# Edge types in eight bins of 63 with overlapping pairs of bins, in place of four quarters of 125

## The reference

```
m    = clifford_linear(h_hc[src] * r_hc[edge_type], msg_w, msg_b)
gate = sigmoid(r_uv @ gate_w.T + gate_b)
m    = m * gate * norm
h_agg = segment_sum(m, dst)          # 206250 edges -> 6250 nodes
```

## Time and profile before

| | us |
|---|---|
| median of 3 runs | 5540.87 (5525.53 to 5540.95) |
| the profiled execution | 5538.96 |
| its span, first to last instruction | 5537.2 |
| first gather of pass one, of pass two | 245.4, 2799.0 |
| last gather of pass one, of pass two | 2766.3, 5436.3 |

### The profile page before, as it was taken

How to read it: one execution, slowest core, us unless ns; L and a number is a source line. 1 busy time by engine, 2 the same in 40 slices (tenths; PEclk the granted TensorE clock), 3 DMA queues, 4 the chain that set the end, 5 groups by cost and what they waited for, 6 DMA issues and landing times.

```text
span 5537.2 us, 71370 instructions
## 1 busy us (share of the span) xinstructions
PE 3935.6 (71%) x21018; PEld 3039.0 (55%) x21018; DVE 3031.5 (55%) x11695; ACT 1615.8 (29%) x6417; POOL 3854.6 (70%) x4302
## 2 busy tenths in 40 slices
PE   6555555555655566555568888888888888888886
PEld 6444444444444444444445666666666666666665
DVE  8845555555555555555545554545545454555545
ACT  3144544445444454454400111111111111111111
POOL 0177777777777777777767777777777777777772
PEclk9577777777777777777789999999999999999998
DMA  4333333333333333333344444444444444444442
GB/s 97 117 94 96 98 97 96 97 96 98 97 96 98 97 96 97 98 96 93 97 110 114 112 112 109 113 106 112 109 111 111 109 112 108 109 110 115 108 108 76
DMA packets 275026, 571.67 MB, mean 103 GB/s; under 512 B 86332, under 2 KB 164377, under 8 KB 274643
## 3 DMA queue, kind: packets, MB, share of 16 engines
q0 software_dynamic: 164640, 456.82, 32.9%
q1 hardware_dynamic: 98162, 101.78, 5.9%
q10 hardware_dynamic: 11840, 8.50, 0.5%
HBM read 539.92 MB, written 26.92 MB: 102 GB/s over the span
## 4 chain that ended last, share of the span: by engine, by line
PE 40%; DVE 31%; another core or an unknown queue 17%; issue 8%; ACT 2%; DMA 1%; SPq 0%; DVEq 0%; PEldq 0%; ACTq 0%
PE psE L707 15%; DVE both L1335 8%; PE psT L688 7%; PE psY L688 6%; DVE work L1409 5%; DVE work L1405 4%; PE psE L901 3%; PE psE L882 2%; ACT work L1073 2%; DVE work L1257 2%; PE psY L664 1%; DVE work L1352 1%; DVE work L1343 1%; DVE st L1466 1%
## 5 line engine op out<-in xcount | busy, mean ns | idle before, releaser
L601 POOL DMA_INDIRECT work<-t_d,srci x3430 | 3276.2, 955 | 1581.8 <-issue 1166.2
L707 PE MATMUL psE<-work,both 128*128 128x257 f32 x6860 | 2172.1, 440 | 796.7 <-issue 308.0
L707 PEld LDWEIGHTS psE<-work,both 128*128 128x128 f32 x6860 | 1364.0, 221 | 1131.1 <-issue 391.1
L1073 ACT ACTIVATE work<-work 128x35 f16<-128x35 bf16 x5145 | 1131.8, 311 | 657.0 <-DVE work L1405 440.7
L1335 DVE TENSOR_SCALAR both<-iof,dstf 128x128 f32<-128x128 f32 x3430 | 817.4, 347 | 29.6 <-remote 16.4
L1405 DVE TENSOR_SCALAR work<-iob,work 128x35 bf16<-128x35 bf16 x1715 | 273.2, 267 | 870.3 <-remote 692.3
L1352 DVE TENSOR_TENSOR work<-work,psT 128x257 f32<-128x257 f32 x858 | 347.4, 420 | 632.4 <-PE psT L688 276.3
L1352 DVE TENSOR_TENSOR work<-work,psY 128x257 f32<-128x257 f32 x857 | 347.3, 420 | 622.8 <-PE psY L688 231.3
L598 POOL MEMSET idle<- 128x640 bf16 x856 | 574.0, 671 | 0.2
L688 PE MATMUL psT<-relb,work 125*128 125x257 bf16 x3381 | 541.8, 283 | 19.5 <-DVE work L1343 18.5
L688 PE MATMUL psY<-relb,work 125*128 125x257 bf16 x3381 | 545.4, 284 | 4.5 <-issue 4.3
(11 more groups left out here) (260 smaller groups left out, 3218.2 us busy)
## 6 DMA issues: line engine op xcount, KB each, us to landing
work<-t_d,srci POOLq DMA_INDIRECT x3430
work<-types_d SPq DMA_DIRECT2D x245, 218.8 KB
both<-acc_d SPq DMA_DIRECT2D x98, 130.0 KB
t_d<-accf SPq DMA_DIRECT2D x7, 910.0 KB, 9.1
acc_d<-work ACTq DMA_DIRECT2D x1, 6370.0 KB
t_d<-accf SPq DMA_DIRECT2D x49, 130.0 KB
X<-in_x SPq DMA_DIRECT2D x1, 6144.0 KB
out<-X SPq DMA_DIRECT2D x6, 896.0 KB
```

The lines of the kernel that those rows point to most:

```text
L601: pool.indirect_dma_start(gath[:, n % RG, :], None, table, bass.IndirectOffsetOnAxis(ap=srci[:, n:n + 1], axis=0)).then_inc(s_g[n % RG], 16)
L707: ins = nc.tensor.matmul(psE[:, b % 2, 0:DW], sel[:, third, k % SG, :], gath[:, n % RG, 0:DW], start=False, stop=(k == C - 1))
L1073: ins = nc.scalar.activation(to_s3[:, n % 2, i, j, :], to_s[:, n % 2, i, :], ACT.Copy, scale=load3[:, b // RB % 2, j, w:w + 1])
```

## The change

The types are sorted into BINS = 8 bins of BIN = 63 types (the last has 59) and not into 4 quarters of 125. The relation table is held as PAIRS = 7 overlapping pairs of neighbouring bins, each pair on PT = 126 partitions (types 63c to 63c + 125), again in three bfloat16 parts. A slot that holds edges of two neighbouring bins is then served by one pair. Counted from the planning functions: before, 539 of the 1715 slots have two visits and the total is 2254; in the changed kernel 2 slots have two and the total is 1717. A visit is three matmuls in both. The one-hot instructions of pass two go from 395 to 493, over 1717 x 128 columns in all where there were 2254 x 128.

What else comes with it:

- `marks` makes 8 masks in place of 4 and finds the bin by a multiplication and a shift.
- `rank` and `places` go block by block, since 8 x 35 = 280 columns of three blocks do not fit a PSUM bank. A new semaphore `s_pl` lets TensorE write the next block's counts only when VectorE has read the last.
- In the group loop a batch is a period of 15 groups. Its steps stood at group 11 (`marks`), 12 (`rank`) and 14 (`places`) of the period before; they stand at 5 (`marks`), 6, 9 and 12 (`rank`), and 9, 12 and 14 (`places`).
- The bfloat16 parts of the table are no longer made ahead of pass one. The gated table goes to DRAM as before; SP loads one pair at a time back into `gw` (`load_pair`, at blocks 3, 7, ..., 27) and VectorE splits it (`parts`, at group 0 of blocks 6, 10, ..., 30).
- `within` tests 7 borders and not 3. `relb` grows by 3 pairs, and to make room `idle`, `digits`, `turn_at` and `st` move or shrink. The memset between gathers has the same shape in a new place.

The core of the diff:

```
-def quarters(b, k):
+def pairs(b, k):
     first = [0] + [lo for lo, hi in turns(b)]
     end = [hi for lo, hi in turns(b)] + [C]
-    return [c for c in range(RK) if first[c] <= k < end[c]]
+    has = [c for c in range(BINS) if first[c] <= k < end[c]]
+    odd = len(has) % 2 and has[-1] == PAIRS
+    return list(range(has[0] - odd, has[-1] + 1, 2))
...
-        relb = sb("relb", [P, 3, RK, DW + 1], BF16)
-        tid = sb("tid", [P, RK])
+        relb = sb("relb", [P, 3, PAIRS, DW + 1], BF16)
+        tid = sb("tid", [P, PAIRS])
...
+            def load_pair(c):
+                q = min(PT, R - BIN * c)
+                if c == 0:
+                    sp.wait_ge(s_relwd, 16)
+                else:
+                    sp.wait_ge(s_split, c)
+                sp.dma_start(gw[0:q, 0:DW], relw_d[BIN * c:BIN * c + q, :]).then_inc(s_pair, 16)
...
-            def rank(r):
-                w = blocks_of(r) * RK * C
-                pe.wait_ge(s_rk, r + 1)
...
+            def rank(b):
+                pe.wait_ge(s_rk, b // RB + 1)
+                if b >= 1:
+                    pe.wait_ge(s_pl, b)
+                if b >= 2 * RB:
+                    pe.wait_ge(s_typ_h, b // RB - 1)
+                mine = marked[:, b % RB, :, :].rearrange("p c k -> p (c k)")
+                nc.tensor.matmul(psT[:, 0, 0:BINS * C], trib[:, :], mine, start=True, stop=True)
+                nc.tensor.matmul(psT[:, 1, 0:BINS * C], oneb[:, :], mine, start=True, stop=True).then_inc(s_rp, 1)
...
-            dve.wait_ge(s_relwd, 16)
-            for part in range(3):
-                link(v.tensor_copy(relb[0:q, part, :, 0:DW], rel_sb[0:q, :, :]))
-                if part < 2:
-                    link(v.tensor_tensor(rel_sb[0:q, :, :], rel_sb[0:q, :, :], relb[0:q, part, :, 0:DW], ALU.subtract))
+            v.memset(relb[:, :, PAIRS - 1, :], 0.0)
...
+            def parts(c):
+                q = min(PT, R - BIN * c)
+                dve.wait_ge(s_pair, 16 * (c + 1))
+                for part in range(3):
+                    ins = v.tensor_copy(relb[0:q, part, c, 0:DW], gw[0:q, 0:DW])
+                    if part < 2:
+                        link(ins)
+                        link(v.tensor_tensor(gw[0:q, 0:DW], gw[0:q, 0:DW], relb[0:q, part, c, 0:DW], ALU.subtract))
+                ins.then_inc(s_split, 1)
...
+            def places(r, i):
+                b, nb = RB * r + i, blocks_of(r)
+                m, at = BINS * C, C * i
+                dve.wait_ge(s_rp, b + 1)
+                flat = before[:, :, :].rearrange("p c k -> p (c k)")
+                mine = marked[:, i, :, :].rearrange("p c k -> p (c k)")
+                link(v.tensor_tensor_scan(flat, ones[:, 0:1].broadcast_to([P, m]), psT[:, 1, 0:m], 0.0, ALU.mult, ALU.add))
+                link(v.tensor_tensor(flat, flat, psT[:, 1, 0:m], ALU.subtract))
+                link(v.tensor_copy(turn_at[:, b, :], before[:, 1:BINS, 0]))
+                link(v.tensor_tensor(flat, flat, psT[:, 0, 0:m], ALU.add))
+                dve.sem_inc(s_pl, 1)
+                link(v.tensor_tensor(flat, flat, mine, ALU.mult))
+                link(v.tensor_reduce(spot[:, at:at + C], before[:, :, :].rearrange("p c k -> p k c"), AX, ALU.add))
+                if i < nb - 1:
+                    return
...
-                        b, g = n // SPB, n % SPB
-                        if b % RB == RB - 1 and b + 1 < NB:
-                            if g == 1:
-                                marks(b // RB + 1)
-                            if g == 4:
-                                places(b // RB + 1)
+                    for r in range(1, RANKS):
+                        if n == SPB * RB * (r - 1) + 5:
+                            marks(r)
+                        for i, j in zip(range(blocks_of(r)), (9, 12, 14)):
+                            if n == SPB * RB * (r - 1) + j:
+                                places(r, i)
+                    for c in range(PAIRS):
+                        if n == SPB * (4 * c + 6):
+                            parts(c)
```

More of the change, by code:

```diff
@@ L48 @@
 RP = R // RK
+BINS = -(-R // BIN)
+PAIRS = BINS - 1
+PT = 2 * BIN
+TO_BIN = -(-(1 << 16) // BIN)
 HT = H // P
@@ L69, in turns @@
     out = []
-    for j in (1, 2, 3):
-        f = j / 4
+    for j in range(1, BINS):
+        f = j * BIN / R
         spread = 4 * sqrt(n * f * (1 - f) + n * f * f)
@@ L87, in visits @@
     out, at = [], 0
-    for c in range(RK):
-        has = [i for i in range(SG) if c in quarters(b, SG * g + i)]
-        if has:
-            out.append((c, has[0], len(has), at))
-            at += len(has)
+    for c in range(PAIRS):
+        i = 0
+        while i < SG:
+            many = 0
+            while i + many < SG and c in pairs(b, SG * g + i + many):
+                many += 1
+            if many:
+                out.append((c, i, many, at))
+                at += many
+            i += many + 1
     return out
@@ L127, in program @@
         accf = sb("accf", [P, NB * W])
-        work = sb("work", [P, 11604])
+        work = sb("work", [P, 11404])
         srci = sb("srci", [P, SLOTS], I32)
@@ L146, in program @@
         o = RG * W
-        H4 = work[:, o:o + 2 * RW].bitcast(BF16).rearrange("p (b c k) -> p b c k", b=RB, c=RK)
-        o += 2 * RW
-        before = work[:, o:o + 4 * RW].rearrange("p (b c k) -> p b c k", b=RB, c=RK)
-        o += 4 * RW
+        marked = work[:, o:o + BINS * RW // 2].bitcast(BF16).rearrange("p (b c k) -> p b c k", b=RB, c=BINS)
+        o += BINS * RW // 2
+        before = work[:, o:o + BINS * C].rearrange("p (c k) -> p c k", c=BINS)
+        o += BINS * C
         good = work[:, o:o + RW]
@@ L235, in program @@
         f2 = work[:, o:o + HT * D].rearrange("p (t n) -> p t n", t=HT)
-        assert o + HT * D <= 11604
+        o += HT * D
+        assert o + 320 <= 11404
+        idle = [accf[:, NB * W - 320:NB * W].bitcast(BF16), work[:, o:o + 320].bitcast(BF16)]
         late = typ[:, :].bitcast(F32)
@@ L254, in program @@
         iob = sb("iob", [P, P], BF16)
-        idle = sb("idle", [P, 640], BF16)
         w1s = sb("w1s", [P, 2, D])
@@ L351, in program @@
         s_rp = sem("s_rp")
+        s_pl = sem("s_pl")
+        s_pair = sem("s_pair")
+        s_split = sem("s_split")
         s_t1 = sem("s_t1")
@@ L544, in _ @@
             for b in range(NB + 2):
+                if b % 4 == 3 and b // 4 < PAIRS:
+                    load_pair(b // 4)
                 if b + 1 < NB:
@@ L597, in gathers @@
                             pool.wait_ge(s_pause, pause - 1)
-                        pool.memset(idle[:, :], 0.0).then_inc(s_pause, 1)
+                        pool.memset(idle[layer], 0.0).then_inc(s_pause, 1)
                     if n >= RG:
@@ L687, in relations @@
                     for part in range(3):
-                        ins = nc.tensor.matmul(psR[n % BANKS][:, 0:DW], oht[0:RP, g % 2, at, :], relb[0:RP, part, c, 0:DW],
+                        ins = nc.tensor.matmul(psR[n % BANKS][:, 0:DW], oht[0:PT, g % 2, at, :], relb[0:PT, part, c, 0:DW],
                                                start=((c, part) == (mine[0][0], 0)), stop=((c, part) == (mine[-1][0], 2)))
@@ L734, in first_pass @@
             def first_pass():
-                rank(0)
+                for i in range(RB):
+                    rank(i)
                 for n in range(NB * SPB + SPB + 6):
@@ L738, in first_pass @@
                     if n < NB * SPB:
-                        if b % RB == RB - 1 and b + 1 < NB and g == 2:
-                            rank(b // RB + 1)
                         for i in range(SG):
                             aggregate(0, SG * n + i)
+                    for r in range(1, RANKS):
+                        for i, j in zip(range(blocks_of(r)), (6, 9, 12)):
+                            if n == SPB * RB * (r - 1) + j:
+                                rank(RB * r + i)
                     if 0 < n <= NB * SPB:
@@ L971, in _ @@
             first_pass()
-            pe.wait_ge(s_rp, RANKS)
+            pe.wait_ge(s_pl, NB)
+            pe.wait_ge(s_split, PAIRS)
             pe.wait_ge(s_so, NB)
@@ L1342, in one_hots @@
                 for c, first, many, at in visits(n):
-                    ins = v.tensor_scalar(oht[0:RP, n % 2, at:at + many, :], types[0:RP, n % 2, first:first + many, :],
-                                          tid[0:RP, c:c + 1], None, ALU.is_equal)
+                    ins = v.tensor_scalar(oht[0:PT, n % 2, at:at + many, :], types[0:PT, n % 2, first:first + many, :],
+                                          tid[0:PT, c:c + 1], None, ALU.is_equal)
                 ins.then_inc(s_oht, 1)
@@ L1374, in marks @@
                 link(v.tensor_tensor(load3[:, r % 2, 2, 0:w], t, ok, ALU.mult))
[L1376 to L1391 removed]
+            def places(r, i):
[13 more added lines that the diff above has]
+                    return
+                w = C * nb
                 link(v.tensor_copy(src_a[:, 0:w], spot[:, 0:w]))
@@ L1415, in first_pass @@
```

(3 more changed lines are left out.)

68 lines of the change are left out of this document (28 added, 40 removed).

## The result

Over 19 runs each on one chip the changed kernel takes 5525.80 us (5503.03 to 5546.23) and the kernel before 5536.73 (5525.53 to 5547.51): ratio 0.9982 [0.9974, 0.9991], a gain of some 10 us or 0.2%. The forecast was 5511, a gain of 28. The profiled execution after is 5539.22 us with a span of 5537.5, some 13 above the median of its own kernel. So the two traces show no difference in the total, and only their parts can be compared.

A forecast was written before the change was run, and what follows sets the result against it. The prediction took both passes to be bound by GpSimd's gathers, plus an 8% tax from TensorE falling behind. From the profiled 5539 us it summed 5539 - 45 + 15 + 1 + 1 = 5511 us, range 5425 to 5575.

The forecast's parts named there:

- the tax: Both passes: time per slot above GpSimd's burst floor, from TensorE falling behind; 0.128 us in pass one, 0.125 in pass two.
- pass two's term, -45: Pass two: 537 fewer visits lighten TensorE by 3.6 us per block, so the pace falls and 45 us go.
- The rounding up from 39 to 45: Pass two: 39 us in proportion, taken as 45 because the first microseconds off TensorE should be worth more.
- 3.6 us per block: Pass two: TensorE time saved by fewer visits, 0.33 us each and 11 per block of 35 slots.
- the stretch without feed-forward: Pass two, 2830 to 2980 us: 7.7 us less TensorE work per block lowers the pace from 1.545 to 1.493.
- Pass one at +15: Pass one: longer sorting on VectorE, chiefly `marks` ahead of `features` at group 5, costs 1 us per batch, 16 times.
- +1 and +1: Start: table split leaves, longer sorting and the accumulator's load cancel it, +1 us; end: `within` grows by 16 instructions, +1.
- The hand-over to `rank`: Pass one: `rank` of a batch's second and third block waits for VectorE's `s_pl`, under 1 us each.
- `places` was put at 3.0 us: Pass one: `places`, 4.1 us once per batch before, now runs three times at 3.0 us, 9.0 in all.
- The first: Rival, pass two: quicker draining of TensorE's backlog takes 130 of 198 us of lateness; 5426 us, chance 0.13.
- The third: Rival, pass one: `marks` ahead of `features` passes 4.8 us per batch to GpSimd, +77 us; 5571 us, chance 0.18.
- The second: Rival, pass two: VectorE's lumps or a falling TensorE clock eat the gain; 5549 us, no change, chance 0.24.

The follow-up runs named there:

- e18: The kernel before without its second visits on TensorE, sorting and one-hots as before, on the slower kind of chip: 5511.51 us, 0.9953 of the kernel before.
- e4: The changed kernel with the 537 second visits done again on TensorE, the result the same: 5461.13 us, 1.0019 of the kernel before.
- e1: The changed kernel with `marks`, `places` and `parts` at the end of VectorE's group and later `rank` one group later: 5444.25 us, 0.9983 of the kernel before.
- e2: The changed kernel with `marks` alone moved to the end of VectorE's group: 5442.73 us, 0.9976 of the kernel before.
- e17: The changed kernel with only the first of the three bfloat16 parts multiplied, on the slower kind of chip: 5477.97 us, 0.9879 of the kernel before.
- e14: The kernel before with twelve gathers to a burst in both passes: 5546.00 us, 1.0162 of the kernel before.
- e15: The changed kernel with twelve gathers to a burst in both passes: 5580.71 us, 1.022 of the kernel before.
- e13: The kernel before with six gathers to a burst in pass two in place of three: 5512.92 us, 1.0101 of the kernel before.
- e16: The changed kernel with six gathers to a burst in pass two in place of three: 5494.84 us, 1.007 of the kernel before.
- e3: The kernel before with `marks` moved to group 5, ahead of `features`: 5457.21 us, 1.0001 of the kernel before.
- e7: The kernel before, unchanged, run again for a profile on a chip of the faster kind: 5149.56 us, one run.

## Why the prediction was wrong

On a chip with the tax both parts moved as forecast in sign. The size of the gain in pass two did not hold, and the whole gain fell from 28 us to 10.

- **The step that failed: the size of pass two's term, -45.** Measured, the visits are worth 26 us (e18; 17 to 35), 17 to 23 by e4 beside e1 and e2, 36 by the two traces of pass two, and none where the gathers run at their floor. With 26 in place of 45 the forecast's own sum gives a gain of 9 us, and 10 was measured. That a lighter TensorE makes pass two faster on such a chip was right. Two parts of the term were too large. The rounding up from 39 to 45, by which the first microseconds are worth more, had no row behind it, and no such effect is seen in the returns of e17 and e18. And the relief was counted in matmuls at full clock, 3.6 us per block. TensorE's busy time per slot went from 1854.60 / 1391 = 1.333 us to 1776.95 / 1412 = 1.258 with the change and to 1766.29 / 1407 = 1.255 in e18, which is only 2.7 us per block. The matmuls that stayed got longer: one of an aggregate takes 408 ns on average before, 416 with the change, 418 in e18 and 439 in e17 (3250 to 5300 us), at a granted clock of 0.94, 0.93, 0.92 and 0.87. With 2.7 the same proportion gives 0.052 x 2.7 / 7.7 x 1582 = 29 us, an estimate inside e18's interval. So the comparison with the stretch without feed-forward is not refuted, but it was a thin basis: from start to start of the gathers the two stretches lie 0.024 to 0.072 us per slot apart in the 12 traces of the slower kind. (The 131 instructions of the changed kernel can't be divided by 150 us, since its pass two begins at 2835 and not at 2830.)
- **Pass one at +15, with +1 and +1.** All of the change but the visits costs 10 us by e4, and 26 - 10 = 16 by e18 and the result. Single traces scatter: pass one from first to last gather is longer with the changed sorting by 37 us in the pair of the result, 31 between e18 and e17, 22 between e14 and e15, 7 between e13 and e16 and 2 between e3 and e4. The term was about right, the reason beside it was not: it was put down to 1 us per batch of lumps that fall through at group 5. e3 put the old lump there and lost nothing, and e2 took the new one away and gained nothing that can be told. The hand-over to `rank` was put at under 1 us each and is some 8 us when it is seen, but e1, which has none of it, is no faster than e2. Which of the added steps costs the 10 to 16 us is open. `places` was put at 3.0 us and takes 3.2.
- **The tax.** The prediction said that GpSimd's floor is the bound and that the tax is TensorE's falling behind "now and then". Both hold, and the parts of the tax, 0.128 and 0.125 us per slot or 220 and 214 us, are near the 200 and 175 us by which a chip without it is faster. What was not asked is why TensorE falls behind. Pauses between moves that have no wait between them were in the trace of the kernel before as well, and would have warned that load is not all of it. That load only sets how fast TensorE recovers from such a stretch is an argument; no run shows it.
- **The rivals.** The first (the tax nearly goes with quicker draining) falls with e17: with three times the relief in all, pass two is still at 1.492. The third (`marks` ahead of `features`) falls with e1 to e3. The second came nearest of the three in time, 5549 against 5526, but the visits did bring a gain, which it had eaten. That VectorE's lumps set the rest of the tax was not tested. The granted clock of pass two went from 0.94 to 0.93, and not to 0.76; in e17 it is 0.87 with TensorE 75% busy, and that kernel is 57 us faster than the changed one. The rule of the Trainium skill (TensorE: Matmul & The Clock Gate, section on HAM oscillation), that pauses bring the low rate back, agrees in direction with 0.94, 0.93, 0.87. What the low rate costs is seen in the longer matmuls of the first point: it took back part of the relief, not all of it.
- **What would show it.** 5150 relation matmuls: 5151. Pace of pass two 1.517: 1.522. Clock 0.92 or above: 0.93. Pace of pass one 1.475: 1.490. Waits moved to the features' transposes: 34 to 81 us. The pace of pass two in the one profiled run bore the forecast out better than the runs did: by the medians the gain is a third of it.

Still open: what makes TensorE and VectorE issue slowly in some sets, whether that is of the chip or of the recording, how much of the tax it accounts for, and why denser gathers make the tax larger. No run tells whether a deeper ring or finer freeing helps there.

## What to carry to other kernels

When an engine falls behind now and then, look in the trace at a run of its instructions that have no wait between them: if they stand far apart, its load is not all of the lateness, and lightening it may return only a fraction (here some 0.15 us per us). Price what an edit takes from TensorE in busy time and not only in matmuls at full clock: here 3.6 us per block counted were 2.7 busy. And where a kernel sits on a floor of one engine, test a change of the floor itself early, and in more than one set of runs: the same edit gave -3.0% in one and +0.7 to +1.0% in another.

## What the runs showed of the hardware

- One program took 5155, 5163, 5453, 5460, 5537 and 5541 us in the result and the five sets, while the runs of one kernel in one set lie within 0.8% of each other. The means of the gather and the product agree: a gather takes 955 ns in the first trace of the kernel before and 954 in set 2 (e7), a product 420 and 421. What differs for them is the time between instructions.
- On the slower kind TensorE issues matmuls often 0.7 or 1.4 us apart, for 1.5 to 9 us at a time, in 10 to 25 of 245 groups of moves, 85% of them in the first two groups of a block. VectorE shows pauses of 1 to 2.5 us within a chain of its own in the changed kernel's first trace.
- On the faster kind TensorE's mean granted clock in pass two was 0.99 for the kernel before, 0.96 for the changed one; on the slower 0.94 and 0.93.
- With the granted clock the mean duration of a matmul moves: one of an aggregate in pass two takes 408 ns at 0.94 (before) and 439 at 0.87 (e17).
